# Who issues the reloads of the kept halves: ScalarE behind its stores, or SyncE

## What is computed

```python
x = x + L0_conv(gn(x), weight)   # depthwise 6x11 filter, lower triangle only (causal mask before and after)
x = x + (gn(x) + bias)           # bias[c, i, j] = table[i - j + n - 1, c], the table from a small MLP
```

## Time and profile before

| | us |
|---|---|
| median of 3 runs | 2590.82 (2589.96 to 2599.15) |
| profiled execution, its own time | 2585.05 |
| its span | 2583.2 |
| steady laps, start to start (992.7, 1298.3, 1604.1) | 305.6 and 305.8 |
| DVE busy in such a lap | 280 |
| DMA, mean over the span | 347 GB/s |

### The profile page before, as it was taken

One profiled execution on the slowest core, in us unless ns is written; L12 is line 12 of the kernel. 1 busy time (PEld: TensorE's weight loads), 2 busy tenths in 40 slices (PEclk: granted clock), 3 DMA queues, 4 the chain that ended last, 5 costly groups with the idle time before them and its releaser, 6 DMA issues.

```text
span 2583.2 us, 74659 instructions
## 1 busy us (share of the span) xinstructions
PE 1919.8 (74%) x28080; PEld 1812.2 (70%) x28080; DVE 2274.1 (88%) x4175; ACT 1649.4 (64%) x3051; POOL 1213.6 (47%) x1988
## 2 busy tenths in 40 slices
PE   4189887878788877877778777787778778899800
PEld 0189887777687777867778677786768778888700
DVE  7789998899988999989988999889998899878846
ACT  2167676766667566666767666676766757787722
POOL 1122235534645455454545446553564545475543
PEclk9989999999999999989989999999998999999955
DMA  9766649999999999999999999999999998898999
GB/s 336 274 237 197 228 147 369 399 359 356 356 405 387 367 349 371 415 351 392 348 371 395 355 379 367 373 394 371 364 361 395 387 361 318 306 364 288 339 379 360
DMA packets 313610, 895.91 MB, mean 347 GB/s; under 512 B 42273, under 2 KB 42273, under 8 KB 311297
## 3 DMA queue, kind: packets, MB, share of 16 engines
q1 hardware_dynamic: 198528, 576.64, 60.9%
q10 hardware_dynamic: 114832, 316.22, 31.4%
HBM read 576.36 MB, written 316.53 MB: 346 GB/s over the span
## 4 chain that ended last, share of the span: by engine, by line
DVE 41%; DMA 26%; PE 12%; issue 10%; ACT 5%; POOL 3%; SPq 1%; ACTq 1%; POOLq 0%; DVEq 0%
DVE entries L837 12%; DMA ring<-in_x 10%; PE psY L1194 10%; DVE kept_c_band L999 7%; DVE XT L807 6%; DVE kept_c_band L824 4%; DMA out<-ring 4%; DVE psY L822 4%; DMA out<-band 3%; DMA out<-kept_c_band 3%; DVE ring L1010 3%; DMA kept_c_band<-in_x 2%; PE psT L1180 2%; ACT junk L684 2%; DVE band L824 2%
## 5 line engine op out<-in xcount | busy, mean ns | idle before, releaser
L1194 PEld LDWEIGHTS psY<-wsplit,XT 128*128 128x128 f16 x25200 | 1551.6, 101 | 377.8 <-DVE XT L807 223.5
L1194 PE MATMUL psY<-wsplit,XT 128*128 128x128 f16 (+5 forms) x25200 | 1581.8, 222 | 308.5 <-DVE XT L807 250.2
L664 ACT CAST XT<-psT 128x512 f16<-128x512 f32 x720 | 406.3, 564 | 492.8 <-PE psT L1180 277.9
L1120 POOL COPY halo<-XT 128x16 f16<-128x16 f16 x720 | 315.5, 438 | 683.9 <-DVE XT L807 674.1
L837 DVE BATCH_NORM_STATS2 entries<-ring 128x6 f32<-128x512 f32 x872 | 551.5, 679 | 79.3 <-DMA ring<-in_x 79.0
L807 DVE TENSOR_TENSOR XT<-psT,XT 128x512 f16<-128x512 f32 x720 | 482.8, 671 | 102.2 <-ACT XT L664 101.7
L1093 POOL TENSOR_TENSOR xn<-xn,mask 128x512 f32<-128x512 f32 (+2 forms) x336 | 381.9, 1137 | 393.8 <-ACT xn L651 340.6
L1180 PE MATMUL psT<-ident,xn 128*128 128x128 f32 x2800 | 470.4, 292 | 122.8 <-POOL xn L1093 80.4
L1129 POOL TENSOR_TENSOR ring<-ring,bias 128x1024 f32<-128x1024 f32 x181 | 408.9, 2261 | 257.2 <-ACT ring L713 256.0
L651 ACT ACTIVATE xn<-kept_c_band,normp 128x512 f32<-128x512 f32 (+2 forms) x496 | 398.4, 803 | 63.7 <-DMA kept_c_band<-in_x 39.1
L1180 PEld LDWEIGHTS psT<-ident,xn 128*128 128x128 f32 x2800 | 308.9, 146 | 132.2 <-POOL xn L1093 64.3
(11 more groups left out here) (81 smaller groups left out, 484.3 us busy)
## 6 DMA issues: line engine op xcount, KB each, us to landing
ring<-in_x SPq DMA_DIRECT2D x628, 512.0 KB, 8.7
out<-ring ACTq DMA_DIRECT2D x282, 512.0 KB, 6.5
kept_c_band<-in_x SPq DMA_DIRECT2D x224, 512.0 KB, 8.2
out<-kept_c_band ACTq DMA_DIRECT2D x224, 512.0 KB, 7.1
band<-in_x SPq DMA_DIRECT2D x48, 1024.0 KB, 11.1
out<-band ACTq DMA_DIRECT2D x45, 1024.0 KB, 9.7
ring<-out SPq DMA_DIRECT2D x90, 512.0 KB, 10.0
bias<-bias_scratch SPq DMA_DIRECT2D x16, 1793.5 KB, 8.8
```

The lines of the kernel that those rows point to most:

```text
L664: nc.scalar.copy(XT[:, n % NB3, 0, 0:np, 2:P + 2], psT[n % NB3][:, 0:np, :]).then_inc(hi_ready, 1)
L1120: nc.gpsimd.tensor_copy(halo[:, t, :, 0:np, :], XT[:, n % NB3, :, 0:np, P:P + 2]).then_inc(halo_out, 1)
L1194: last = nc.tensor.matmul(psY[m][:, 0:rows, o + lo_c:o + hi_c], XT[:, m, xp, i, 2 - sh:2 - sh + P], wsplit[:, c, wp, K * sh:K * sh + rows, ...
```

## The change

The reloads of the laps from the third on (7 laps with 28 halves, 196 of the 224 reload DMAs) leave SP's program. ACT issues them at the end of its own position `reload_pos`, behind its stores of that position, with the wait for the store on the DMA instruction itself. The first group's 28 halves, in `load_first`, stay with SP. Sizes, buffers and all other positions stay as they are; the semaphores are the same ones.

```diff
-                        for blk in KEPT:
-                            for h in range(2):
-                                if reload_pos(blk, h) == n and gb > 0:
-                                    load_kept(gb, blk, h)
@@ scalar engine
+            def load_kept_anew(g, blk, h):
+                c, b = blk[:2]
+                half = blk[5] // 2
+                act.wait_ge(kept_stored[(blk, h)], 16 * g)
+                act.dma_start(part(kept[(c, b)], blk, half * h, half), part(xv[chan(g, c), b], blk, half * h, half)
+                              ).then_inc(kept_loaded[blk], 16)
@@ scalar engine, end of position n in stage()
+                    if do_b and gb > 0:
+                        for blk in KEPT:
+                            for h in range(2):
+                                if reload_pos(blk, h) == n:
+                                    load_kept_anew(gb, blk, h)
```

## The result

The changed kernel takes 2630.2 us (median of 4 runs, 2626.5 to 2633.8) against 2590.4 for the kernel before (4 runs, 2587.25 to 2599.15). The ratio is 1.015, interval 1.0131 to 1.0168. I had forecast 2594 with a range to 2628. The profiled execution took 2633.8 us, its span is 2632.1; the one of before had 2585.05 and 2583.2. The two profiles thus differ by 49 us where the medians differ by 40; some 9 us in the comparison of the traces are the spread of single executions, and a term of 1 us per lap is not to be trusted from them.

What follows compares the result with a forecast made beforehand. DVE and DMA were taken as near-bounds. Per lap -5.1 - 1.1 + 5.1 + 4.7 + 1.4 - 4.5 absorbed = +0.5; seven laps give +3.5, hence 2588.6 profiled and 2594 us as median, 8-in-10 range 2562 to 2628.

Steps and rivals of the forecast that it cites:

- SP's hold-up: SP waits 220.2 us for stores of kept halves, 44 us per lap, delaying ring loads behind; the change removes this.
- Its gain, 6.2 us a lap: DVE's waits for ring loads at position 13 (5.1 us) and behind position 55 (1.1 us) end.
- Position 10: ACT waits for the third reload's store, its CAST 5.1 us late in the mean, cancelling DVE's gain at position 13.
- Position 19 and its absorption: ACT is 4.7 us late before tile 22's CAST; DVE's later load waits of 7.9 us absorb all but 0.5.
- the signs that I had set: Absorption is wrong if DVE's gaps near positions 34 and 40 stay 4.9 and 3.1 us though position 19 lost 5.
- The slower rival: Position 19's stall of 4.7 us a lap is not absorbed because loads slip too: 2624, or 2633; chance 0.30.
- Position 55, 1.4 us against 1.1 won: ACT's CAST behind three reloads comes 1.4 us late, against 1.1 us of DVE's load wait saved; net 0.3.
- Seven laps: The third to the ninth lap carry the change; each was given the same +0.5 us, +3.5 in all.
- Issues, 69 us beneath idle time: 28 reload issues a lap on ACT at 0.351 us, 69 us in all, cost nothing given 102 us idle a lap.
- The bytes' queue, zero with plus or minus 3 us a lap: Moving 196 reloads, 103 MB, from SP's queue to ACT's costs zero, plus or minus 3 us a lap; landing 7.1 us.

Runs made afterwards that it cites:

- The edit that brings most of the gain without the move: Kernel before, all reloads on SP, last half of position 10 issued one position later and that of 55 two later: 2594.2 against 2592.7, 1.0004.
- the run with waits and issues: Kernel before, ACT also waiting at the 196 places and issuing 196 DMAs of 128 bytes, reloads still on SP: 2615.1 against 2592.7, 1.008.

## Why the prediction was wrong, step by step

- **SP's hold-up goes:** right. No wait of SP on kept stores is left among the rows above, and position 13 waits for no load.
- **Its gain, 6.2 us a lap:** the two waits of DVE did go (4.8 and 1.6 us in the mean), but the waits for ring loads at positions 40 and 64 grew by 1.6 and 2.4, and over five laps only 10.6 us less were waited for ring loads where 31 were forecast. I had read two gaps of DVE as time won. The edit that brings most of the gain without the move is worth nothing (1.0004); it is not proof that the lap takes any advance back, for it also loads two halves later.
- **Position 10:** right in size. ACT's wait there was 4.7 us in the mean (forecast 5.1), against 4.8 that DVE no longer lost at position 13.
- **What stands ahead of position 10, put at nothing:** DVE is 3.5 us late at tile 12 already, and 0.2 where channel 0's reloads are SP's. With 196 DMAs of 128 bytes it is 2.1, so more than half of it is the mere issue of DMAs at positions 6 and 9. The sum had no term for it.
- **Position 19 and its absorption:** the size of the wait was wrong, and the absorption half right. ACT waited 0.9 us instead of 4.7, as its last store landed after 6.4 us in the mean instead of 11.9, when five ring loads no longer left at once beside it (a reading that no run isolates; where SP keeps the loads, the wait is 4.7 to 6.3). What had been lost by then, 4.0 us at tile 18, was down to 1.9 at tile 54, so half of it stayed, where the sum left 0.5 of 4.7. By the signs that I had set, the gaps at 34 and 35 shrank (4.2 to 2.6) and the one at 40 grew (3.0 to 4.6). The slower rival had the right price, 2624 to 2633, by luck: it rested on a stall at position 19 of 4.7 us, and this was 0.9.
- **Position 55, 1.4 us against 1.1 won: the step that failed first.** I took the landing of the store from the trace of before (6.3 us), though the change itself puts reloads close ahead of that store and in its queue; it took 9.6. The wait was 5.3 us on ACT and 3.9 on DVE, and 3.3 instead of 0.9 us followed on the ring load at 64. Of the 6.7 us that a steady lap loses, 4.8 lie behind tile 54. The DMA engines are full behind this place too (1.02 from 1170 to 1230). What is missing are waits of DVE that a delay could use up. I had even said under the slower rival that reloads stand ahead of ACT's stores, and priced it only there, at 1.3 us each, for ring stores. The run with 51 and 54 on SP gives 14 us back.
- **"Seven laps": the second step that failed.** The sum has 0.5 us for each. The seventh has no statistics loads, hence no wait for a load that takes a delay back, and ACT has 44 us to spare instead of 102. It lost 11.6 us, 11.0 of them in DVE's waits for CASTs; the run with that lap on SP gave 14 back. The windows of this lap could have been read before.
- **Issues, 69 us beneath idle time, cost nothing:** both wrong. They took 122.6 us (40 of the 196 took over 1 us, 53 us together), and 196 small ones cost 0.35% (9 us) alone. ACT's idle time in the lap is not where these issues are: they stand ahead of a CAST that DVE waits for.
- **ACT's waits for reloaded halves, in no term:** 34.0 us in five laps before, 1.7 changed. What this relief brought DVE, no run shows.
- **The bytes' queue, zero with plus or minus 3 us a lap:** for the sum of seven laps the run with waits and issues leaves some 18 us, 2.6 a lap, at the edge of my bound and all on the bad side. A reload landed after 8.3 us in the median, where I took 7.1 and SP's queue had 8.2. Part of the 18 us is the late store at position 55. How they divide between the later starts of the reloads and the queue's order was not separated. That the reloads' starts matter is shown only for the blocked ones (31 us for two positions).

The Trainium skill (DMA: Bandwidth & Descriptors, section "Issuing engines are not separate DMA queues") says that transfers interleave on the same 16 engines whoever started them and that only the sequencer's time is saved. These runs agree that no bandwidth was won (365 to 367 GB/s a lap against 374). They show in addition two things that depend on the issuer: the wait stands in its program order (0.73%), and a store lands sooner or later (6.0 or 9.6 us) with who issues the reloads around it and thus when.

None of these versions beats the kernel before. The nearest, with two halves loaded later by SP, can't be told from it.

## What to carry to other kernels

A DMA that must wait belongs on an engine that has nothing urgent behind the wait; idle time of an engine over a lap is no measure of that, what stands behind the instruction is. When a change adds transfers to a queue, price the landings of the stores behind them anew, and don't read them from the old trace. Before counting on a stretch to absorb a delay, add up the waits of the same engine in it: 7.2 us of them took back some 2 of 4 us here, 2.5 us took back 1.6 and then gave 2.4. And a lap that differs from the steady ones (the last, without loads) wants a sum of its own.

## What was not expected of the hardware

Issuing one DMA from ACT took 0.33 us at the shortest and 2.34 us at the longest, mean 0.63 over 196, in a kernel whose DMA share is 0.97; ACT's whole time in DMA issues rose from 307 to 432 us. An extra transfer of 128 bytes took as long to issue as one of 0.5 MB (median 0.45 and 0.39 us). And kept stores of the same size, at the same place of the lap, landed after 6.0 us with the reloads of positions 51 and 54 on SP's queue and after 9.6 with them on ACT's own, where two of them also started 5 us later; the number of transfers was the same.
